# A ring of eight places for the one-hot matrices in place of four, in a two-layer graph network on one core

## The chip, the cores and the metric

The kernel runs on one core of one Trainium2 chip. Times are device microseconds (us). The time before is 308.18 us, the median of three runs (306.78 to 308.36). The trace comes from one further execution, which took 307.07 us.

## The reference, cut to what matters

There are 1024 nodes with 512 features each and 16384 edges, given as `src` and `dst` and sorted by `dst`. The first layer is a masked attention, the second a graph convolution over the same edges:

```
h    = max(layernorm(x), 0)
q, k, v = h @ Wq + bq, h @ Wk + bk, h @ Wv + bv
adj[src, dst] = 1
a    = q @ k.T / sqrt(512), where adj is 1, and -1e6 elsewhere
x    = x + softmax(a) @ v
h    = max(layernorm(x), 0)
h    = agg(h @ W1 + b1)                 # agg: sum over edges, weights dinv[src] * dinv[dst], and loops
h    = relu(batchnorm(h))
x    = x + agg(h @ W2 + b2)
```

Both `adj` and `agg` can be had from one matrix of counts, cnt[dst, src], which says how many edges lead from each source to each target.

## The kernel before, in words

**The counts.** The matrix of counts is made by TensorE (PE). The 128 chunks of 128 edges each are turned into pairs of one-hot matrices: `src_oh` (128 edges x 512 columns, L705) and `dst_oh` (128 edges x 128 columns, for 64 targets in each half of the sources, L707). A matmul of the two (L1055) adds a chunk's edges to the counts of one group of 64 targets. There are 16 groups (`NW`), taken in the order `ORDER`. Since the edges are sorted by target, a group needs only the chunks between two bounds, read into registers (`bounds_of`). A group is worked off in rounds: first one round of two chunks (`LEAD`), then a loop with three chunks a round (`UNROLL`). For groups 3 to 9 ScalarE (ACT) makes the two leading source one-hots instead (`lead_onehots`, L473 and L476), and VectorE (DVE) only the targets' part.

**The ring.** DVE makes the one-hots of a round in one place of a ring, PE uses them. The ring has `RING = 4` places; the place of round k is `k & (RING - 1)`, on both engines. DVE waits until the semaphore `onehots_used` has reached k + 1; PE adds `RING` to it once at the start, and each round's last matmul adds 1. So DVE can be at most four rounds ahead. PE waits until `onehots` has reached k + 1.

**What else runs in this stage.** Between the groups PE makes other products, in the order of `ahead`: before group i it makes the items of `ahead[i]`, such as a block of v (12 matmuls, L989 to L991), a turned block of h (L1023) or a block of q. ACT copies each item's high part from PSUM (L491, L488), DVE the low part (L688, L684). DVE takes the low parts of `ahead[i-2]` just before the one-hots of group i. ACT also copies each group's counts from PSUM (L464), and PE starts group i only once the counts of group i - 2 are copied (`c16`) and, for groups 3 to 9, the leading one-hots are there (`lead_made`). GpSimd (POOL) makes the shifted targets of each group (`drel`, L365) and the columns of the leading chunks (L370). Before group 0 PE has made the turned weights `WT` and three of the four blocks of M = Wq Wk^T; the fourth (`early[11]`) comes after group 0, and the first four blocks of turned h (`early[12:]`) come after group 1.

**Order.** Each engine's order is written out by hand. All waits are on semaphores; nothing is planned by a scheduler.

**Memory.** `src_oh` follows `qk_raw` in a region of 32 KiB a partition; the region behind it is that of `WT`, in which `w_row` lies from 12 KiB on, and `hrow` from 16 KiB on. `dst_oh` shares a region of 4 KiB with `p16`; `hnT` shares another of 4 KiB with `res` and `res_h`.

After the counts come the last blocks of q, the scores and the softmax row by row, the products with v and W1, both aggregations and the product with W2. They use nothing of the ring.

Of the kernel before, what the change touches and what calls it, by code (L numbers as in the profile page):

```python
# [17 lines left out]
P = 128  # L18
N = 1024
# [3 lines left out]
KC = D // P  # L23
NCH = E // P
HALF = 512
# [5 lines left out]
UNROLL = 3  # L31
PAD = 4
ROUNDS = NW * (2 + NCH // UNROLL)
RING = 4
ORDER = (14, 15) + tuple(range(14))
ITEM_BANKS = 6
LOADS = 2
# [14 lines left out]
F32R = mybir.dt.float32r  # L52
BF16 = mybir.dt.bfloat16
F16 = mybir.dt.float16
# [4 lines left out]
def gnn_kernel(nc, x, src, dst, Wq, bq, Wk, bk, Wv, bv, W1, b1, gamma, beta, W2, b2, out):  # L59
    ctx = ExitStack()  # L60

    def sb(name, shape, dt, where=ctx):
        return where.enter_context(nc.sbuf_tensor(name, shape, dt))

    def shared(*groups):

        made = []
        for g in groups:
            s = ExitStack()
            made += [sb(name, shape, dt, s) for name, shape, dt in g]  # L70
            s.close()
        return made

    def hold(name, kib):
        sb(name, [P, 256 * kib], F32)
# [9 lines left out]
        [("qh", [P, NT, 2, KC * P], F32R)],  # L85
        [("qk_raw", [P, 2, KC, D], F32), ("src_oh", [P, RING, UNROLL, HALF], BF16)])
    hold("region_qh", 32)
    WT, pT, h16, h16T, w_row, _, w2, _, hrow, _, w2_raw, g32 = shared(
        [("WT", [P, 2, 2, KC, D], F32R)],
        [("pT", [P, 2, NT, P], F32R), ("h16", [P, 2, D], F16), ("h16T", [P, 2, KC, P], F16), ("w_row", [P, D], F32),  # L90
         ("unused", [P, D], F32), ("w2", [P, 2, KC, D], F32R)],
        [("pT_place", [P, 2, 2, NT, P], F32R), ("hrow", [P, KC, D], F32)],
        [("pT_place2", [P, 2, 2, NT, P], F32R), ("w2_raw", [P, 2, KC, D], F32)],
        [("g32", [P, KC, N], F32)])
# [17 lines left out]

    p16T, drel_second = shared([("p16T", [P, 2, NT, P], F16)], [("drel_second", [P, NW // 2, NCH + PAD], F16)])
    hold("region_p16T", 4)
    dst_oh, p16 = shared([("dst_oh", [P, RING, P, UNROLL], BF16)], [("p16", [P, 2, N], F16)])
    hold("region_dst_oh", 4)
    ecol = sb("ecol", [P, NCH + PAD], F32)
    hnT, res, res_h = shared(
        [("hnT", [P, 2, KC * P], F32R)],
        [("res", [P, HALF], F32R), ("res_h", [P, 2, P], F32R)])  # L120
    hold("region_hnT", 4)
    bias_row = sb("bias_row", [P, 2, D], F32)
    ncol = sb("ncol", [P, NCH + PAD], F32)
    lead_col = sb("lead_col", [P, NW, LEAD], F32)
# [49 lines left out]
    S = {n: ctx.enter_context(nc.semaphore(n)) for n in sem_names}  # L174
# [13 lines left out]
    item_bank = lambda item: start.get(item, final.get(item, 2 + (items.index(item) - len(start)) % ITEM_BANKS))  # L188
    last_in = lambda b, end: max([n for n, other in enumerate(items[:end], 1) if item_bank(other) == b] + [0])

    drel = lambda i: (drel_first if i < NW // 2 else drel_second)[:, i % (NW // 2), :]
    row_of = lambda t: T[:, t // 2, t % 2 * D:(t % 2 + 1) * D] if t < KC else hrow[:, t - KC, :]

# [434 lines left out]
    def _(dve):  # L628
# [70 lines left out]
        def chunks_of(i, c, count, src=True):  # L699

            k = dve.snap(made, min_val=0, max_val=ROUNDS)
            slot = k & (RING - 1)
            dve.wait_ge(S["onehots_used"], k + 1)
            for j in range(count if src else 0):
                dve.tensor_scalar(src_oh[:, bass.ds(slot, 1), j, :].rearrange("p a n -> p (a n)"), iota[:, :],  # L705
                                  ecol[:, bass.ds(c + j, 1)], None, ALU.is_equal)
            dve.tensor_tensor(dst_oh[:, bass.ds(slot, 1), :, 0:count].rearrange("p a n u -> p (a n) u"),  # L707
                              iota_w[:, :, 0:count],
                              drel(i)[:, bass.ds(c, count)].rearrange("p (o u) -> p o u", o=1).to_broadcast(
                                  [P, P, count]), ALU.is_equal).then_inc(S["onehots"], 1)  # L710
            dve.reg_add(made, made, 1)

        def onehots(i, bounds):

            first, end = bounds & (NCH - 1), bounds >> 8
            dve.wait_ge(S["drel_ready"], i + 1)
            chunks_of(i, first, LEAD, not ACT_LEADS <= i < ACT_LAST)
            with dve.Fori(first + LEAD, end, UNROLL) as c:
                chunks_of(i, c, UNROLL)
# [266 lines left out]
    def _(pe):  # L986
# [11 lines left out]
        for a in range(2):  # L998
            m = pe.transpose(bank(1)[:, a * P:(a + 1) * P], ext[:, a:a + 1].to_broadcast([P, P]), ident[:, :])
        m.then_inc(S["ext_ps"], 1)  # L1000
        pe.sem_inc(S["onehots_used"], RING)
        used = pe.alloc_register("used")
        pe.reg_mov(used, 0)

# [41 lines left out]
        def bounds_of(i):  # L1046
            return pe.value_load(lohi[0:1, ORDER[i]:ORDER[i] + 1], min_val=256, max_val=257 * NCH)

        def chunks(i, count, first):

            k = pe.snap(used, min_val=0, max_val=ROUNDS)
            slot = k & (RING - 1)
            pe.wait_ge(S["onehots"], k + 1)
            for j in range(count):
                m = pe.matmul(ps[:, i % 2, :], dst_oh[:, bass.ds(slot, 1), :, j].rearrange("p a n -> p (a n)"),  # L1055
                              lead_oh[:, i % 2, j, :] if first and ACT_LEADS <= i < ACT_LAST else
                              src_oh[:, bass.ds(slot, 1), j, :].rearrange("p a n -> p (a n)"), start=first and j == 0,
                              stop=False, skip_group_check=True)
            m.then_inc(S["onehots_used"], 1)
            pe.reg_add(used, used, 1)  # L1060

        def counts(i, bounds):

            if i >= 2:
                pe.wait_ge(S["c16"], 2 * (i - 1))
            if ACT_LEADS <= i < ACT_LAST:
                pe.wait_ge(S["lead_made"], LEAD * (i - ACT_LEADS + 1))
            first, end = bounds & (NCH - 1), bounds >> 8
            chunks(i, LEAD, True)
            with pe.Fori(first + LEAD, end, UNROLL):  # L1070
                chunks(i, UNROLL, False)
            pe.matmul(ps[:, i % 2, 0:32], zerob[:, :], zerob[:, 0:32], start=False, stop=True,  # L1072
                      skip_group_check=True).then_inc(S["c_done"], 1)
# [17 lines left out]
        for i in range(NW):  # L1091
            for item in ahead[i]:
                make(item)
            now = bounds
            if i + 1 < NW:
                bounds = bounds_of(i + 1)
            counts(i, now)
            if i == 0:
                make(early[11])
            if i == 1:  # L1100
                for item in early[12:]:
                    make(item)
        make(("q", 1, 0))
# [172 lines left out]
```

## Time and profile before

| | us |
|---|---|
| time, median of three runs | 308.18 |
| the profiled execution's own time | 307.07 |
| its span, first to last instruction | 305.2 |
| PE busy | 294.4 (96%) |
| DVE busy | 207.2 (68%) |
| ACT busy | 160.0 (52%) |
| POOL busy | 58.2 (19%) |
| one-hot matmuls, L1055 from `src_oh`, 131 records | 33.0 |
| source one-hots on DVE, L705, 135 records | 40.0 |
| target one-hots on DVE, L707, 35 of 55 records in the largest group | 14.8 |

The granted clock of TensorE is 0.999 of full speed. The profiled execution lasts 1.87 us longer than its span. Starts are in us from the span's start. A row of the timeline merges neighbouring instructions of a line: the start, the time they cover, the engine, the line, what is written and read, how many, and in brackets the engine's idle time before them and what ended it. The bound of a wait named there is inferred by the profiler. Some matmul records are missing (for instance 131 of 135 one-hot matmuls from `src_oh` are there).

### The profile page before, as it was taken

Reading aid. Unit: us, or ns where it says so; the run is one execution under the profiler, and the core shown is the slowest. Engines: PE = TensorE matmul, PEld = TensorE weight load, DVE = VectorE, ACT = ScalarE, POOL = GpSimd, SP = SyncE. Lnnn points to the kernel's source line nnn. Section 1 sums busy time; section 2 is a strip of 40 time slices with the busy share of each in tenths; the row PEclk is TensorE's granted clock in tenths of the full one; section 3 lists DMA queues with packets and bytes.
Section 4 is the critical chain, followed back from the end, with each engine's and each line's share of the span. In section 5 each row is a group of like instructions: output and inputs, shape, how many; then the busy total and the mean of one; then the engine's idle time right before and its main releaser. Section 6 shows DMA issues by size and latency. Waiting matters only on the chain.

```text
span 305.2 us, 4839 instructions
## 1 busy us (share of the span) xinstructions
PE 294.4 (96%) x1339; PEld 227.2 (74%) x1345; DVE 207.2 (68%) x458; ACT 160.0 (52%) x266; POOL 58.2 (19%) x103
## 2 busy tenths in 40 slices
PE   7999889899999999999999999999999999999995
PEld 6777356466665888888888888887888888878884
DVE  3899989999978557965748575568345388276311
ACT  3999967989546546445444554367523044342000
POOL 5351454000000530022131320203010044100000
PEclk9999999999999999999999999999999999999999
DMA  6816040000600309434362625313102000000321
GB/s 250 317 34 176 1 141 0 1 0 2 207 0 3 69 3 240 81 91 95 79 151 40 147 43 104 69 36 69 34 20 52 0 3 0 0 2 0 111 98 69
DMA packets 42312, 21.67 MB, mean 71 GB/s; under 512 B 35760, under 2 KB 36016, under 8 KB 42288
## 3 DMA queue, kind: packets, MB, share of 16 engines
q1 hardware_dynamic: 41744, 20.33, 26.2%
q10 hardware_dynamic: 544, 1.05, 0.9%
q8 instruction: 12, 0.20, 0.3%
q14 instruction: 12, 0.10, 0.1%
HBM read 10.88 MB, written 2.10 MB: 43 GB/s over the span
## 4 chain that ended last, share of the span: by engine, by line
PE 81%; DVE 7%; ACT 4%; DMA 3%; issue 3%; DVEq 1%; ACTq 0%
PE ps L989 18%; PE ps L991 18%; PE ps L990 18%; PE ps L1242 10%; PE ps L1165 8%; PE ps L1055 8%; DMA p16T<-p 2%; DMA qk_raw<-L_gnn_Wk_in 1%; DVE src_oh L705 1%; PE ps L1023 1%; DVE T L809 1%; DVE WT L688 1%; DVE smx L813 1%; DVE dst_oh L707 1%; ACT T L531 1%
## 5 line engine op out<-in xcount | busy, mean ns | idle before, releaser
L705 DVE TENSOR_SCALAR src_oh<-iota,ecol 128x512 f16 x135 | 40.0, 349 | 3.3 <-PE ps L1055 2.8
L1055 PE MATMUL ps<-src_oh,dst_oh 128*128 x131 | 33.0, 381 | 3.9 <-DVE dst_oh L707 3.0
L1165 PE MATMUL ps<-cnt,qh 128*128 128x512 f32 x128 | 30.1, 391 | 0.3 <-ACT cnt L575 0.3
L1055 PEld LDWEIGHTS ps<-src_oh,dst_oh 128*128 x135 | 13.3, 103 | 21.6 <-issue 12.2
L1242 PE MATMUL ps<-qh,cnt 128*128 128x512 f32 x128 | 29.3, 390 | 0.0
L1165 PEld LDWEIGHTS ps<-cnt,qh 128*128 128x128 f32 x128 | 23.9, 188 | 5.6 <-DVE qh L868 0.7
L1242 PEld LDWEIGHTS ps<-qh,cnt 128*128 128x128 f32 x128 | 23.9, 188 | 5.2 <-DVE vb L970 0.3
L991 PE MATMUL ps<-v,pT 128*128 128x512 f32 x64 | 25.0, 390 | 0.0
L989 PE MATMUL ps<-v,pT 128*128 128x512 f32 x64 | 24.9, 390 | 0.0
L990 PE MATMUL ps<-v,pT 128*128 128x512 f32 x64 | 24.9, 390 | 0.0
L989 PE MATMUL ps<-hT,qh 128*128 128x512 f32 x64 | 24.9, 389 | 0.0
L990 PE MATMUL ps<-hT,qh 128*128 128x512 f32 x64 | 24.9, 389 | 0.0
L991 PE MATMUL ps<-hT,qh 128*128 128x512 f32 x64 | 24.9, 389 | 0.0
L403 POOL TENSOR_SCALAR lnb<-bnag 128x1 f32<-128x1 f32 x8 | 7.2, 899 | 81.4 <-DVE bnag L842 81.4
L464 ACT ACTIVATE cnt<-ps 64x512 int16<-64x512 f32 x32 | 18.9, 590 | 5.7 <-PE ps L1072 5.1
L982 DVE SCALAR_TENSOR_TENSOR xt<-ps,dinv,x 128x512 f32<-128x512 f32 x8 | 5.7, 747 | 17.1 <-PE ps L1242 17.1
L531 ACT ACTIVATE T<-T,smx 128x1024 f32<-128x1024 f32 x8 | 9.2, 1154 | 13.7 <-DVE smx L814 13.7
L831 DVE TENSOR_SCALAR pT<-p16T 128x1024 fp32r<-128x1024 f16 x8 | 5.5, 693 | 15.5 <-DMA p16T<-p 15.5
L559 ACT ACTIVATE hnT<-h16T 128x512 fp32r<-128x512 f16 x8 | 5.1, 632 | 20.2 <-DMA h16T<-h 20.2
L498 ACT ACTIVATE T<-zerob,fill 128x1024 f32<-128x1024 bf16 x8 | 9.1, 1147 | 12.4 <-DVE p L821 12.4
L809 DVE COPY_PREDICATED T<-adj,ps 128x1024 f32<-128x1024 int16 x8 | 10.6, 1321 | 7.1 <-PE ps L991 7.1
L707 DVE TENSOR_TENSOR dst_oh<-iota_w,drel_first 128x384 f16 (+1 forms) x35 | 14.8, 422 | 0.6 <-PE ps L1055 0.6
(186 smaller groups left out, 685.0 us busy)
## 6 DMA issues: line engine op xcount, KB each, us to landing
xt<-x_in SPq DMA_DIRECT2D x16, 256.0 KB, 3.2
out<-xt SPq DMA_DIRECT2D x8, 256.0 KB, 2.1
qk_raw<-L_gnn_Wk_in ACTq DMA_DIRECT2D x2, 512.0 KB, 4.9
qk_raw<-L_gnn_Wq_in SPq DMA_DIRECT2D x2, 512.0 KB, 6.8
wB_raw<-L_gnn_Wv_in SPq DMA_DIRECT2D x2, 512.0 KB, 9.0
wB_raw<-L_gnn_W_in SPq DMA_DIRECT2D x2, 512.0 KB, 4.2
w_raw<-L_gnn_W_in SPq DMA_DIRECT2D x2, 512.0 KB, 4.5
bias_row<-L_gnn_b_in SPq DMA_DIRECT2D x2, 256.0 KB, 4.7
```

The costliest lines, as they stand in the source:

```text
L464: act.activation(cnt16[rows, a * KC:(a + 1) * KC, w // 2, :], ps[a * WIN:(a + 1) * WIN, i % 2, :].rearrange("p (s n) -> p s n", n=P), ACT. ...
L498: act.activation(T[:, t % 2, :], zerob[:, 0:1].to_broadcast([P, N]), ACT.Identity, bias=fill[:, t:t + 1]).then_inc(S["mask_set"], 1)
L531: act.activation(T[:, t % 2, :], T[:, t % 2, :], ACT.Exp, bias=smx[:, 1, t:t + 1], scale=SCALE, accum_out=smx[:, 2, t:t + 1]).then_inc(S[" ...
L705: dve.tensor_scalar(src_oh[:, bass.ds(slot, 1), j, :].rearrange("p a n -> p (a n)"), iota[:, :], ecol[:, bass.ds(c + j, 1)], None, ALU.is_ ...
L707: dve.tensor_tensor(dst_oh[:, bass.ds(slot, 1), :, 0:count].rearrange("p a n u -> p (a n) u"), iota_w[:, :, 0:count], drel(i)[:, bass.ds(c ...
L809: dve.copy_predicated(T[:, t % 2, :], adj[:, t % ADJ, :], ps[:, 2 * (t % 2):2 * (t % 2) + 2, :].rearrange("p a n -> p (a n)")).then_inc(S[ ...
L989: pe.matmul(out_, stat(1), mov(0), start=first, stop=False)
L990: pe.matmul(out_, stat(0), mov(1), start=False, stop=False)
L991: return pe.matmul(out_, stat(0), mov(0), start=False, stop=last)
L1055: m = pe.matmul(ps[:, i % 2, :], dst_oh[:, bass.ds(slot, 1), :, j].rearrange("p a n -> p (a n)"), lead_oh[:, i % 2, j, :] if first and ACT ...
L1165: m = pe.matmul(bank(g), qh[:, d, a, c * P:(c + 1) * P], cnt[:, d, n * HALF:(n + 1) * HALF], start=(d == 0 and a == 1), stop=last)
L1242: m = pe.matmul(bank(t), cnt[:, d, t * P:(t + 1) * P], qh[:, d, a, :], start=(d == 0 and a == 1), stop=last)
```

## The change

The ring has eight places from group 2 on; groups 0 and 1 still use four. PE adds 4 to `onehots_used` at the start and 4 more after group 1, before it makes `early[12:]`. `src_oh` grows from 12 to 24 KiB a partition and so reaches over the end of its region into the first 8 KiB of that of `WT`. `dst_oh` grows from 3 to 6 KiB; its region and that of `hnT` become one of 8 KiB, and `ecol` now lies behind it.

```diff
-RING = 4
+RING = 8
+FIRST_RING = 4
...
-    dst_oh, p16 = shared([("dst_oh", [P, RING, P, UNROLL], BF16)], [("p16", [P, 2, N], F16)])
-    hold("region_dst_oh", 4)
+    dst_oh, p16, hnT, _, res, res_h = shared(
+        [("dst_oh", [P, RING, P, UNROLL], BF16)],
+        [("p16", [P, 2, N], F16), ("hnT", [P, 2, KC * P], F32R)],
+        [("p16_place", [P, 2, N], F16), ("res", [P, HALF], F32R), ("res_h", [P, 2, P], F32R)])
+    hold("region_dst_oh", 8)
     ecol = sb("ecol", [P, NCH + PAD], F32)
-    hnT, res, res_h = shared(
-        [("hnT", [P, 2, KC * P], F32R)],
-        [("res", [P, HALF], F32R), ("res_h", [P, 2, P], F32R)])
-    hold("region_hnT", 4)
...
+    ring_of = lambda i: FIRST_RING if i < 2 else RING
...
         def chunks_of(i, c, count, src=True):
-            slot = k & (RING - 1)
+            slot = k & (ring_of(i) - 1)
             dve.wait_ge(S["onehots_used"], k + 1)
...
-        pe.sem_inc(S["onehots_used"], RING)
+        pe.sem_inc(S["onehots_used"], FIRST_RING)
...
         def chunks(i, count, first):
-            slot = k & (RING - 1)
+            slot = k & (ring_of(i) - 1)
             pe.wait_ge(S["onehots"], k + 1)
...
             if i == 1:
+                pe.sem_inc(S["onehots_used"], RING - FIRST_RING)
                 for item in early[12:]:
                     make(item)
```

## Rows read from the trace of the kernel before

**Rows 1.** Busy time by stretch: PE, PEld, DVE, ACT, POOL (instructions), clock, DMA share, GB/s.
```profile
27.40:42.50 15.10, 12.77 (x54) 6.71 (x53) 13.91 (x49) 14.11 (x33) 4.60 (x13) 1.00 0.31 80
...
60.00:87.00 27.00, 26.85 (x122) 17.69 (x123) 26.05 (x83) 20.13 (x40) 0.00 (x0) 1.00 0.18 59
...
99.50:180.00 80.50, 80.50 (x356) 66.22 (x355) 53.38 (x97) 41.66 (x55) 19.53 (x21) 1.00 0.44 95
```

**Rows 2.** Waits from 15 to 100 us: total us, times, longest.
```profile
PE ps L1055 <- DVE dst_oh L707: 3.0, 9, 0.5
DVE src_oh L705 <- PE ps L1055: 2.8, 5, 0.9
...
PE ps L1055 <- ACT cnt L464: 0.7, 1, 0.7
DVE dst_oh L707 <- PE ps L1055: 0.6, 1, 0.6
```

**Rows 3.** Timeline of DVE, groups 2 and 3.
```profile
29.38 0.87 DVE L705 TENSOR_SCALAR src_oh<-iota,ecol 128x512 f16 x3
...
30.51 0.87 DVE L705 TENSOR_SCALAR src_oh<-iota,ecol 128x512 f16 x3
...
32.27 0.88 DVE L705 TENSOR_SCALAR src_oh<-iota,ecol 128x512 f16 x3 [0.56 <-PE ps L1055]
...
40.34 0.88 DVE L705 TENSOR_SCALAR src_oh<-iota,ecol 128x512 f16 x3
...
42.18 0.38 DVE L707 TENSOR_TENSOR dst_oh<-iota_w,drel_first 128x256 f16 x1 [0.63 <-PE ps L1055]
...
46.71 1.01 DVE L705 TENSOR_SCALAR src_oh<-iota,ecol 128x512 f16 x3
47.65 0.50 DVE L707 TENSOR_TENSOR dst_oh<-iota_w,drel_first 128x384 f16 x1
```

**Rows 4.** Timeline of PE, groups 2 and 3.
```profile
31.63 2.97 PE L1055 MATMUL ps<-src_oh,dst_oh 128*128 x13
...
41.81 0.83 PE L1055 MATMUL ps<-src_oh,dst_oh 128*128 x3 [0.33 <-DVE dst_oh L707]
...
46.29 2.95 PE L1055 MATMUL ps<-src_oh,dst_oh 128*128 x12
```

**Rows 5.** Timeline of POOL beside group 3.
```profile
43.31 5.54 POOL L365 TENSOR_SCALAR drel_second<-dcol 128x132 f16<-128x132 f16 x8
```

**Rows 6.** Chain of work that ended last, groups 3 and 5: start, us, what.
```profile
48.41 0.83 PE ps L1055 x3
...
54.70 1.15 ACT lead_oh L476
...
56.53 0.38 PE ps L1055
```

**Rows 7.** Timeline of DVE, groups 14 and 15.
```profile
90.98 0.75 DVE L684 SCALAR_TENSOR_TENSOR qh<-ps,uw,qh 128x512 fp32r<-128x512 f32 x1 [0.73 <-ACT qh L488]
...
94.87 0.88 DVE L705 TENSOR_SCALAR src_oh<-iota,ecol 128x512 f16 x3 [0.73 <-PE ps L1055]
...
98.10 0.41 DVE L707 TENSOR_TENSOR dst_oh<-iota_w,drel_second 128x384 f16 x1
```

**Rows 8.** Timeline of PE, groups 14 and 15.
```profile
95.13 2.04 PE L1055 MATMUL ps<-src_oh,dst_oh 128*128 x8
...
97.10 0.62 PE L1023 MATMUL ps<-ident,uw 128*128 128x128 f32 x4
...
98.81 0.83 PE L1055 MATMUL ps<-src_oh,dst_oh 128*128 x3 [0.54 <-DVE dst_oh L707]
```

**Rows 9.** Timeline of PE's weight loads, groups 5 and 15.
```profile
56.30 0.23 PEld L1055 LDWEIGHTS ps<-lead_oh,dst_oh 128*128 x2 [0.66 <-issue]
57.14 0.41 PEld L1055 LDWEIGHTS ps<-src_oh,dst_oh 128*128 x3 [0.61 <-issue]
...
97.65 0.26 PEld L1055 LDWEIGHTS ps<-src_oh,dst_oh 128*128 x2 [0.17 <-issue]
```

## The prediction, made before the changed kernel was run

> **What bounds the kernel now.** Start with the busy time by stretch [rows 1]. From 99.5 to 180 us PE is busy for 80.50 of 80.50 us, and nothing of the ring is used there: whatever comes earlier at 99.5 us comes earlier at the end. In the stage of the counts this differs from stretch to stretch. From 27.4 to 42.5 us, which is group 2 (12 rounds, the longest group), DVE is busy for 13.91 of 15.10 us and PE for only 12.77. From 60 to 87 us PE is busy for 26.85 of 27.00 us. So the question is only where PE waits for one-hots, and which of these waits a longer ring takes away.
>
> The waits [rows 2] give the ceiling: PE waits 3.0 us for DVE's one-hots, nine times, and DVE waits 2.8 + 0.6 = 3.4 us for a place. These are two sides of different things. A deeper ring makes DVE no faster; it only lets it use time in which it now stands. So the timeline has to say for each wait of DVE whether PE later had to wait for what DVE lost in it.
>
> **Group 2.** DVE starts its rounds while PE still makes two blocks of v. The rounds start at 29.38 and 30.51 us (1.13 apart), and the next, the fifth, not at 31.64 but at 32.27 [rows 3]: the four places are full, and PE takes the first at 31.63 [rows 4]. From there DVE has no gap to the last round, begun at 40.34 (7 rounds on, (40.34 - 32.27) / 7 = 1.153 us each), and PE waits 0.33 us for the last one, which it starts at 41.81 [rows 3, 4]. So DVE bounds the group from the stall to its end. With eight places the fifth round starts at 31.64: 32.27 - 31.64 = 0.63 us is gained, and PE's last round comes at 41.18. PE still waits for most rounds of the group, since a round costs DVE 1.15 us and PE three matmuls of some 0.22 us ((2.97 - 0.38) / 12 from the thirteen of [rows 4], where 0.38 is one matmul [rows 6]). Of the waits of PE, those in this group stay almost entirely.
>
> The gap of 0.63 us at 42.18, which the trace puts down to PE [rows 3], I don't count: it stands before the first round of group 3, and the place it needs was left by the round of PE four before, more than two such rounds before the one at 41.81 [rows 4]. It comes after the loop's end and the read of the next bounds, so I take it to be the sequencer's, and it stays. Were it the ring's after all, it would bring up to 0.14 us (next paragraph).
>
> **Group 3.** PE's last round starts at 48.41 [rows 6], 0.25 us after DVE's last one-hot of it ends (47.65 + 0.50 = 48.15) [rows 3]. DVE's 0.63 us puts it at 47.78. PE's own bound is close: its rounds would begin at 46.29 - 0.63 = 45.66, and nine matmuls of 0.22 us later it could start the last at 47.64 [rows 4]. So the group yields between 0.63 and 48.41 - 47.64 = 0.77 us in all. The spare 0.14 us depends on POOL. Its eight L365 instructions take 43.31 to 48.85 [rows 5], and beside them a round takes DVE 48.15 - 46.71 = 1.44 us instead of 1.13 [rows 3]. If DVE is earlier by 0.63 us, half a round less lies beside POOL, worth up to 0.15 us. I take half: 0.70 us after group 3.
>
> Here the Trainium skill has a rule that says otherwise (SBUF — State Buffer, "Who interferes with whom"): DVE and GpSimd share a port pair that is locked for a whole instruction, and the loser waits. The trace agrees that they hinder each other (1.44 against 1.13 us). By that rule the price goes by POOL instruction and not by time side by side: the same eight meet DVE, wherever it stands, and group 3 gives 0.63 us and not 0.70.
>
> **Groups 4 to 13.** The 0.70 us must be carried by every engine that PE waits for. PE starts group 5 at 56.53, released by ACT, whose second half of the leading one-hots ends at 54.70 + 1.15 = 55.85 [rows 6] (the wait list names another ACT instruction, L464, for these 0.7 us [rows 2]). ACT came to this work from the block of v that PE had just ended, so it moves with PE; the wait stays and the gain passes through. From 60 to 87 us PE has 0.15 us idle in all [rows 1] and needs nothing of DVE that is not there with a margin of over 1 us: DVE is busy for 26.05 of 27 us there, and its own start is also earlier. Here the new places bring nothing and cost nothing. The one risk is ACT, 20.13 us busy.
>
> **Groups 14 and 15.** DVE waits for ACT's copy of a q block until 90.98, which moves with PE. Then it loses 0.73 us to the full ring before the third round of group 14 at 94.87, and so its last one-hot ends at 98.10 + 0.41 = 98.51 [rows 7], and PE, 0.54 us idle, starts its last round at 98.81 [rows 8]. Without the stall the one-hots are ready at 98.51 - 0.73 = 97.78 on the old clock, which is before PE could use them. What then bounds PE is its own sequencer: in group 5, where the data had been there, the next round's weights were loaded 57.14 - 56.30 = 0.84 us after the first round's [rows 9]. From 97.65 [rows 9] this gives 98.49, so 0.3 us earlier than 98.81. Its queue could be better filled than in group 5: two matmuls of 0.22 us give 98.09, so 0.7 us. With neither, 0. I take 0.35, near the first, the nearest row. Group 14's eight matmuls take 2.04 us where 7 x 0.22 + 0.38 = 1.92 would do [rows 8]: between 0 and 0.1, I take 0.05.
>
> **The edits themselves.** The masks with 7 or 3 are the same instruction on each engine. The added semaphore increment on PE is one sequencer operation before the four turned blocks of h; it stands in PE's own queue between instructions that wait for nothing new, and I price it at 0, at most one gap such as the 0.17 us in [rows 9]. It is no new wait either: DVE's group 2 comes behind the low parts of `early[12:]`, which PE makes after the increment. The same order keeps the new places free: they lie over the first 8 KiB of `WT`, read last by the fourth block of M, after group 0. The moved buffers cost nothing, since no instruction or DMA is added. Whether DVE writes as fast over the region's end the trace cannot show; the nearest rows are the round of 1.13 us and the slowest, 1.44 us, and I take 1.13, since POOL explains the other.
>
> **Sum.** 0.63 + 0.07 + 0.05 + 0.35 = 1.10 us. From the profiled execution's own 307.07 us this gives 305.97 us (span 305.2 to 304.1). The median shown, 308.18, is 0.36% above that execution; less the same 1.10 us it is 307.1 us. That is the forecast. From the terms' ends: at least 0.63, at most 0.77 + 0.1 + 0.7 = 1.57, and 1.73 if DVE's pitch in group 2 were 1.13 instead of 1.153 over seven rounds (0.16).
>
> **The rivals.**
> - *Only a part arrives.* Group 2's 0.63 us is kept, but the end gives nothing because PE's sequencer, or the copies by ACT of the counts of group 13, take DVE's place; or ACT, whose work fills three quarters of 60 to 87 us [rows 1], keeps its own time and eats some of the 0.70. Gain 0.3 to 0.65, time 307.7. For it: an `issue` gap stands before the weights of nearly every drained round [rows 9]. Against it: ACT's work hangs on what PE has ended.
> - *More arrives.* All upper ends and the pitch: 1.73 us, time 306.5. For it: PE's queue would be fuller in group 15. Against it: four terms at their best at once.
> - *Nothing.* The Trainium skill (Perfetto Trace Analysis, "Identifying the Most-Contended Engine") says to speed up the engine with the highest share first, which over the span is PE. As a mechanism: PE has so little idle time after 60 us (0.15 of 27 us [rows 1]) that an earlier DVE finds no room, if the gain at 41.8 us is taken back by another wait before 60. Time 308.2. The stretch of group 2, where DVE leads, speaks against it.
> - *Slower.* DVE's writes to places 4 to 7 of the longer buffer take the slow round of 1.44 us. Groups 0 and 1 have two rounds each, so group 2 starts in place 4 and has eight of its twelve rounds in such places: 8 x (1.44 - 1.13) = 2.5 us, less 0.63, so slower by 1.9 us at group 2, and about 0.5 us of this given back at the end: 309.6. It decides from 0.08 us a round on (0.63 / 8). No row shows a speed that depends on the address; the only slow rounds have POOL beside them [rows 5].
>
> **Chances.** Forecast 0.60, a part only 0.20, more 0.11, nothing 0.05, slower 0.04. Half a per cent, about what a measurement can tell from no change, is 1.5 us. The forecast lies within it; the case of more crosses it, and the forecast crosses it if its terms are near their upper ends (a sixth of its chance): 0.11 + 0.10 = 0.21 for faster, 0.04 for slower, 0.75 for the same. For the range: the median less 1.73 is 306.4 and less nothing 308.2; the three runs of before lie 1.58 us apart (306.78 to 308.36), and the median of another three can sit lower by half of that. So 305.8 to 308.3.
>
> **What would show it.** In the trace after: no idle time of DVE before its fifth round of group 2, PE's last round of that group near 41.2 us and PE still waiting some 0.3 us before each; group 3's last round near 47.7; group 5 still released by ACT, now near 55.8; no wait of DVE for PE at group 14; PE's group 15 ending 1.1 us earlier, with an idle gap by `issue` and not by DVE. The prediction is wrong if DVE's rounds in group 2 are over 1.2 us apart, if the 0.70 us at 48 us has shrunk by 60 or by 90 us, or if the gap at 42.18 us goes.

## The result

The changed kernel takes 305.77 us (median of six runs, 304.32 to 306.05), the kernel before 307.62 us in the same comparison (six runs, 306.78 to 308.36). The ratio is 0.9924, 95% interval [0.9904, 0.9945]: faster by 0.8%, some 2.3 us. The start of the program varies by up to 1.5 us from execution to execution (see below), so these few runs give the size only roughly: the two medians alone differ by 1.85 us, while the traces, counted from the end of group 1, show 2.57 us. Two executions, one of the kernel before (601 us) and one of the kernel "changed, all v early" (1688 us), were slow by far and are left out of all ratios. Forecast were 307.1 us, at least 305.8, and most likely "the same". The direction was right. The size forecast, 1.10 us, was less than half of it, and 0.7 us came at a place where the prediction had nothing.

Line numbers have moved by one: DVE's one-hots, L706 and L708, are the L705 and L707 of before; PE's one-hot matmul L1055 is L1056, L989 to L991 are L990 to L992, and a group's closing matmul of 32 columns, L1072, is L1073.

Busy time by stretch, columns as in [rows 1]:

```profile
27.40:42.50 15.10, 13.52 (x58) 7.43 (x58) 14.44 (x53) 14.62 (x36) 4.56 (x12) 1.00 0.28 78
...
60.00:87.00 27.00, 27.00 (x124) 17.62 (x124) 26.48 (x83) 19.69 (x41) 0.00 (x0) 1.00 0.18 59
```

PE has gained 0.75 us of work in the first stretch (in part the first matmuls of what follows group 2, which now begin inside it), and from 60 to 87 us it is as full as before. The waits from 15 to 100 us, which answer to [rows 2]:

```profile
PE ps L1056 <- DVE dst_oh L708: 2.0, 7, 0.3
...
DVE src_oh L706 <- PE ps L1056: 0.7, 2, 0.4
```

DVE waited 2.8 us for a place before, five times, and now waits 0.7 us, twice.

DVE in group 2, which answers to [rows 3]: the fifth round (31.51) follows the fourth (30.39) after 1.12 us, without a gap, and so on to the last (39.42).

```profile
31.51 0.87 DVE L706 TENSOR_SCALAR src_oh<-iota,ecol 128x512 f16 x3
...
39.42 0.87 DVE L706 TENSOR_SCALAR src_oh<-iota,ecol 128x512 f16 x3
...
41.14 0.37 DVE L708 TENSOR_TENSOR dst_oh<-iota_w,drel_first 128x256 f16 x1 [0.52 <-PE ps L1056]
```

PE in groups 2, 3, 14 and 15, which answers to [rows 4, 8]:

```profile
23.63 0.18 PE L1073 MATMUL ps<-zerob 128*128 128x32 bf16 x1
...
40.89 0.83 PE L1056 MATMUL ps<-src_oh,dst_oh 128*128 x3 [0.29 <-DVE dst_oh L708]
...
45.30 2.75 PE L1056 MATMUL ps<-src_oh,dst_oh 128*128 x12
...
93.88 1.89 PE L1056 MATMUL ps<-src_oh,dst_oh 128*128 x8
...
96.10 1.56 PE L1056 MATMUL ps<-src_oh,dst_oh 128*128 x5
```

The twelve matmuls of group 3 now run through (2.75 us, 2.95 before), and so do the eight of group 14 (1.89 us, 2.04 before). The five of group 15 don't: they take 1.56 us where 4 x 0.22 + 0.38 = 1.26 would do, so a pause of some 0.3 us is left between its two rounds, where 0.54 us was.

**A clock that doesn't scatter.** The start of the span is no good origin: group 1 ends anywhere from 23.6 to 25.0 us after it in the traces of this study, whatever the kernel, and that is most of the scatter between runs. The table takes all from the closing matmul of group 1 (23.63 above), by the starts of these closing matmuls (128x32, from `zerob`) in the timelines of PE. The entry of a group is the start of its own closing matmul. "After" is the end of the span less that of group 15, so all that comes behind the counts. "v2 early" and the like are explained with their experiments.

| kernel | ratio to before [95%] | group 2 | group 3 | group 13 | group 14 | group 15 | after |
|---|---|---|---|---|---|---|---|
| before | | 18.74 | 25.34 | 71.36 | 73.26 | 75.73 | 205.7 |
| the same again | 1.0017 [1.0002, 1.0033] | 18.77 | 25.33 | 71.40 | 73.31 | 75.78 | 205.6 |
| changed | 0.9924 [0.9904, 0.9945] | 17.92 | 24.26 | 70.23 | 71.98 | 73.86 | 205.0 |
| the same again | 0.9908 [0.9885, 0.9931] | 17.93 | 24.29 | 70.26 | 72.02 | 73.90 | 205.0 |
| depth 4, eight places | 0.9987 [0.9970, 1.0004] | 18.77 | 25.35 | 71.42 | 73.33 | 75.80 | 205.1 |
| depth 5, eight places | 0.9914 [0.9890, 0.9938] | 17.92 | 24.28 | 70.30 | 72.05 | 73.90 | 205.1 |
| depth 8 in groups 2, 3 | 0.9941 [0.9919, 0.9962] | 17.92 | 24.33 | 70.29 | 72.20 | 74.67 | 205.1 |
| depth 8 from group 12 | 0.9952 [0.9930, 0.9975] | 18.75 | 25.15 | 71.18 | 72.93 | 74.82 | 205.1 |
| before, ecol behind hnT | 0.9970 [0.9953, 0.9987] | 18.78 | 25.34 | 71.45 | 73.36 | 75.83 | 205.1 |
| changed, hnT 32 bytes off | 0.9940 [0.9919, 0.9960] | 17.92 | 24.33 | 70.30 | 72.05 | 73.94 | 205.7 |
| changed, hnT 64 bytes off | 0.9932 [0.9909, 0.9955] | 17.92 | 24.24 | 70.30 | 72.06 | 73.90 | 205.8 |
| changed, v2 early | 0.9979 [0.9962, 0.9997] | 19.62 | 25.71 | 71.87 | 73.63 | 75.47 | 205.1 |
| before, v2 early | 1.0085 [1.0056, 1.0114] | 21.56 | 27.64 | 73.72 | 75.63 | 78.10 | 205.7 |
| changed, all v early | 0.9984 [0.9958, 1.0010] | 19.63 | 25.97 | 71.94 | 73.69 | 75.58 | 205.0 |
| changed, DVE late | one run | 20.17 | 26.69 | 72.69 | 74.44 | 76.33 | 205.0 |

The change gives 75.73 - 73.86 = 1.87 us in the counts and 205.7 - 205.0 = 0.7 us behind them, where nothing uses the ring.

### The profile page after: what moved, and what is told of

The parts are those of the page before. It is cut to its first block, busy times and chain, and to the rows that moved or that the text cites. A ratio compares the mean times of both kernels' runs of the same rounds, so it can differ in the third digit from the quotient of the medians.

```text
span 302.5 us, 4846 instructions
## 1 busy us (share of the span) xinstructions
PE 293.5 (97%) x1345; PEld 227.1 (75%) x1345; DVE 206.5 (68%) x458; ACT 159.8 (53%) x266; POOL 58.2 (19%) x103
## 3 DMA queue, kind: packets, MB, share of 16 engines
q10 hardware_dynamic: 544, 1.05, 0.9%
## 4 chain that ended last, share of the span: by engine, by line
PE 88%; DVE 6%; issue 2%; DMA 1%; ACT 1%; DVEq 1%; ACTq 0%
PE ps L990 20%; PE ps L991 20%; PE ps L992 20%; PE ps L1244 10%; PE ps L1056 9%; PE ps L1167 8%; DMA qk_raw<-L_gnn_Wk_in 1%; PE ps L1024 1%; DVE src_oh L706 1%; DVE WT L689 1%; DVE T L810 0%; DVE cnt L875 0%; DVE smx L814 0%; DVE p L822 0%; DVE dst_oh L708 0%
## 5 line engine op out<-in xcount | busy, mean ns | idle before, releaser
L706 DVE TENSOR_SCALAR src_oh<-iota,ecol 128x512 f16 x135 | 40.1, 350 | 1.2 <-PE ps L1056 0.7
L1056 PE MATMUL ps<-src_oh,dst_oh 128*128 x135 | 33.4, 381 | 2.5 <-DVE dst_oh L708 2.0
L1056 PEld LDWEIGHTS ps<-src_oh,dst_oh 128*128 x135 | 13.3, 103 | 19.8 <-issue 9.7
L992 PE MATMUL ps<-v,pT 128*128 128x512 f32 x64 | 24.9, 389 | 0.0
L991 PE MATMUL ps<-v,pT 128*128 128x512 f32 x64 | 24.9, 389 | 0.0
L990 PE MATMUL ps<-v,pT 128*128 128x512 f32 x64 | 24.9, 389 | 0.0
L990 PE MATMUL ps<-hT,qh 128*128 128x512 f32 x64 | 24.9, 389 | 0.0
L991 PE MATMUL ps<-hT,qh 128*128 128x512 f32 x64 | 24.9, 389 | 0.0
L992 PE MATMUL ps<-hT,qh 128*128 128x512 f32 x64 | 24.9, 389 | 0.0
L708 DVE TENSOR_TENSOR dst_oh<-iota_w,drel_first 128x384 f16 (+1 forms) x35 | 14.6, 416 | 0.5 <-PE ps L1056 0.5
```

The source lines that it names most:

```text
L990: pe.matmul(out_, stat(1), mov(0), start=first, stop=False)
L991: pe.matmul(out_, stat(0), mov(1), start=False, stop=False)
L992: return pe.matmul(out_, stat(0), mov(0), start=False, stop=last)
```

## The experiments

**Is it the ring at all, and how much is scatter?** Both kernels once more, unchanged.

> The kernel before once more, unchanged, so that two profiles of it stand beside that of the change. The sum of the prediction gave 1.1 us; the two traces show 1.98 us at the end of the counts (last matmul of group 15 starts at 97.49 where it started at 99.47) and 2.7 us over the span. Theory A (all of it comes from the ring): here group 15 ends within 0.2 us of 99.5 again, group 2 shows the fifth-round gap of about 0.56 us, and the rounds after it are again 1.15 us apart. Theory B (part of it is scatter between executions): group 15 ends earlier or later by 0.5 us or more, or the rounds are 1.13 us apart. Time: same as before, ratio 0.998 to 1.002.

> The changed kernel once more. Starts are taken from the end of group 1, which lies at 23.6 to 25.0 us in the six traces so far. If the 1.9 us in the counts are the ring's, group 15 ends 73.9 us after group 1 again (75.7 to 75.8 in the two traces of the kernel before and in the one with depth 4), and the rounds of group 2 are 1.13 us apart (1.15 in those three). If that was scatter, 74.3 or more, or 1.15. Ratio to before about 0.992.

Every entry of the table repeats within 0.1 us. The 1.87 us are no scatter, nor is the 0.7 us behind; the ratio of the kernel before to itself, 1.0017 with an interval that leaves out 1, shows that a whole run is known to some 0.2% only. So the experiments are read by the table and not by their ratios.

**Depth or layout.**

```diff
+    short = lambda i: 0 if i < 2 else 4
...
-            dve.wait_ge(S["onehots_used"], k + 1)
+            dve.wait_ge(S["onehots_used"], k + 1 + short(i))
```

This is depth 4: DVE may run only four rounds ahead, though the ring has eight places. For depth 5 `short` gives 3 in place of 4, for depth 8 in groups 2 and 3 alone it is `0 if i < 4 else 4`, and for depth 8 from group 12 on `0 if i < 2 or i >= 12 else 4`.

> The changed kernel with its eight places and its memory, but from group 2 on DVE waits until it is at most four rounds ahead, as before. It tells the depth from the layout. If the depth does it all: the time of before, ratio 0.998 to 1.002, group 15's end at about 99.5 us, DVE's stalls at the fifth round of group 2 (0.6 us) and at the third round of group 14 (0.7 us) back, rounds in group 2 1.15 us apart. If places over the turned weights or the moved buffers have a share, that share stays: rounds of 1.13 us after the stall, and group 2 earlier by 0.16 us than before.

> Eight rounds ahead in groups 2 and 3 only, four from group 4 on. The gain up to the end of group 3 should be kept as in the change: group 3's last matmul (of 32 columns) at about 47.9 us against 49.1. At the end of the counts, if the terms of the prediction are apart from one another, 1.2 of the 1.98 us: group 15's end near 98.2. Time ratio about 0.996. If the first gain is lost again later (theory: it is only the place where DVE waits), group 15 ends at 99 or later.

> Four rounds ahead until group 11, eight from group 12 on. Only the terms at the end: the prediction had 0.40 us for them (0.05 + 0.35), the two traces show 0.8 us (0.21 in group 14 and 0.52 to 0.58 in group 15). So group 3 ends as before (49.1), group 15 at 98.7 if 0.8 is right, at 99.1 if 0.4 is. Time ratio 0.997 to 0.999.

With depth 4 the counts are those of before to 0.1 us, so the places over the turned weights cost and bring nothing there. The two partial kernels split the gain. Groups 2 and 3 give 75.73 - 74.67 = 1.06 us. The kernel with the depth from group 12 on is 75.73 - 74.82 = 0.91 us ahead at the end, but 0.2 us of that is there at group 3 already (25.15, where the other kernels with four rounds ahead have 25.33 to 25.35), before it differs from them. It is not the depth's: in this one trace DVE's rounds beside POOL fell out shorter. From group 13 on the deep ring gives (75.73 - 71.36) - (74.82 - 71.18) = 0.73 us, the same as the 0.74 of the changed kernel, and so the 0.8 us of the expectation was near and the 0.4 of the prediction too small. The gain of groups 2 and 3 passes through groups 4 to 13 undiminished (25.34 - 24.33 = 1.01 there, 71.36 - 70.29 = 1.07 at group 13). But the depth-4 kernel is 0.6 us faster than before behind the counts. No expectation had that, and the next kernels ask for its cause.

**The 0.7 us behind the counts.** After the softmax each of the eight row blocks of h is multiplied by W1: twelve matmuls a block on the three lines L989 to L991, with a piece of `hnT` (the turned h, high or low part) as the stationary operand, the one that is loaded as weights. Their durations, min/median/max ns, with the first and the last start, in the kernel before:

```profile
L990 PE MATMUL ps<-wB,hnT x32: 392/396/396, 138.2 to 233.9; 128*128 128x512 f32 x32
L991 PE MATMUL ps<-wB,hnT x32: 395/396/397, 138.4 to 234.2; 128*128 128x512 f32 x32
```

and in the changed one:

```profile
L990 PE MATMUL ps<-wB,hnT x32: 389/389/389, 135.9 to 231.1; 128*128 128x512 f32 x32
```

The lines that are not shown have the same. 96 of them at 7 ns less make 0.67 us. As the profiler models the ends of matmuls, the starts count more: those of one block are (140.51 - 137.94) / 11 = 0.234 us apart in the kernel before, and (140.59 - 138.10) / 11 = 0.226 us in the first of the three kernels below, which also has 389 ns. The diff moved ecol, 528 bytes a partition, from ahead of hnT to behind it; the allocation puts hnT at byte 216736 before (32 off a multiple of 128) and at 216192 after (a multiple of 128). Three kernels change only that:

```diff
 # before, ecol behind hnT
-    ecol = sb("ecol", [P, NCH + PAD], F32)
...
     hold("region_hnT", 4)
+    ecol = sb("ecol", [P, NCH + PAD], F32)
 # changed, hnT 32 bytes off (64 bytes: [P, 16])
-    dst_oh, p16, hnT, _, res, res_h = shared(
+    dst_oh, p16, _, hnT, _, res, res_h = shared(
...
-        [("p16", [P, 2, N], F16), ("hnT", [P, 2, KC * P], F32R)],
+        [("p16", [P, 2, N], F16), ("skew", [P, 8], F32), ("hnT", [P, 2, KC * P], F32R)],
```

> The kernel before, ring of four, with ecol (528 bytes) declared behind the region of hnT and not ahead of it. hnT then starts at a multiple of 64 bytes a partition (216192) and not 32 bytes off one (216736). Theory A: the 96 matmuls with hnT as the stationary operand, 396 ns each in the kernel before and 389 in the changed one and in that with depth 4, cost 7 ns more because of this offset; then they take 389 ns here, the rows of the softmax come 13.60 us apart and not 13.69, and the end lies 0.5 to 0.7 us nearer to group 1's end, 280.8 against 281.4, while the counts stay at 75.7. Theory B: they got faster through the ring or something else in the change; then all stays as before. Ratio 0.998 by A, 1.000 by B.

> The changed kernel with 32 unused bytes between p16 and hnT, so that hnT starts 32 bytes off a multiple of 64 again; nothing else differs. Theory A (the offset): the hnT matmuls take 396 ns, the rows come 13.69 us apart, and the end lies 0.5 to 0.6 us later than in the changed kernel, 279.4 after group 1's end against 278.9; the counts stay at 73.9. Theory B (some other effect of the layout): 389 ns, 13.60 and 278.9.

> The changed kernel with 64 unused bytes between p16 and hnT: hnT starts at a multiple of 64 bytes that is not one of 128 (216256). If 64 bytes are the step that matters, the hnT matmuls take 389 ns and the rows come 13.60 us apart, as in the changed kernel; if it is 128, 395 ns and 13.69, as with the 32 bytes.

The kernel before with ecol behind:

```profile
L989 PE MATMUL ps<-wB,hnT x32: 389/389/389, 138.1 to 233.3; 128*128 128x512 f32 x32
```

The changed one with 32 bytes, and with 64:

```profile
L990 PE MATMUL ps<-wB,hnT x32: 392/395/396, 136.2 to 231.9; 128*128 128x512 f32 x32
```
```profile
L990 PE MATMUL ps<-wB,hnT x32: 393/396/398, 137.2 to 233.0; 128*128 128x512 f32 x32
```

The offset is shown as the cause, by taking it from the kernel before and by giving it to the changed one, where nothing but hnT moves: the column "after" goes to 205.1 with the one and back to 205.7 and 205.8 with the others, and the counts don't move. My guess of 64 bytes as the step was wrong: 64 off a multiple of 128 costs the same 7 ns. The 0.7 us have nothing to do with the ring, and a reordered declaration alone gives 205.7 - 205.1 = 0.6 us (the ratio of 0.9970 says 0.9 us, within what a ratio is known to).

**How deep, and why the rounds' pitch changed.** The pitch is the time from one round's start to the next. Between the stall of [rows 3] and the end of group 2 the rounds of before are 1.153 us apart, those of the changed kernel (39.42 - 31.51) / 7 = 1.130.

> Eight places, DVE at most five rounds ahead from group 2 on. In group 2 only the fifth round waited for a place, and PE takes the first round just then, so one place more should be enough: group 2 ends 17.9 us after group 1, as with eight. The rounds after it tell two theories of the pitch apart. A: DVE's sequencer lost its lead over the engine at the stall, and works at 1.15 us a round when it has none; without a stall the pitch is 1.13, as with eight. B: the pitch depends on the distance to a place that PE is reading; with five it stays near 1.15 and group 2 ends at 18.1. At groups 14 and 15 one place more takes the 0.73 us stall away but perhaps not all: group 15's end between 73.9 and 74.3. Ratio 0.992 to 0.994.

Depth 5 is depth 8 in every entry, within 0.1 us. Its rounds in group 2 are 1.13 us apart (31.66 to 40.70, eight rounds). So five rounds ahead are enough for this order of the work. A ring of five places was not built; with the place taken as `k & (RING - 1)`, eight is the next count that can be. For the pitch it left one question, answered by a stall without a short ring:

```diff
+            if i == 2:
+                dve.wait_ge(S["item_ps"], nth(("v", 0, 0)))
             onehots(i, now)
```

> The changed kernel, in which DVE waits before its first round of group 2 until PE has made the block v0, some 1.4 us later than it would start by itself. It still may run eight rounds ahead and no place is ever missing. Theory A (DVE's sequencer loses its lead at any stall and then needs 1.15 us a round): the rounds of group 2 come 1.15 us apart though the ring is deep, and the group ends 1.6 to 1.7 us later than in the changed kernel (17.9 after group 1's end): 19.5 to 19.6. Theory B (the pitch belongs to the ring of four places ahead): 1.13 us apart, group 2's end at 19.3.

```profile
29.54 0.62 DVE L706 TENSOR_SCALAR src_oh<-iota,ecol 128x512 f16 x2 [1.81 <-PE ps L994]
30.38 0.88 DVE L706 TENSOR_SCALAR src_oh<-iota,ecol 128x512 f16 x3
...
41.94 0.88 DVE L706 TENSOR_SCALAR src_oh<-iota,ecol 128x512 f16 x3
```

(41.94 - 30.38) / 10 = 1.156 us with eight places ahead. So the pitch goes with a stall and not with the depth: a stall costs its own length and then 0.02 to 0.03 us for each round until the end of the group (one trace; the six other traces of group 2 with four rounds ahead show the same 1.15 after their stall). Nor is it PE that slows DVE by waiting right behind it, since in the changed kernel PE does so for the last five rounds and DVE keeps to 1.13. That DVE's sequencer has lost its lead over the engine is the reading that fits; no row shows the lead itself. The group ended 2.25 us late and not 1.7, since DVE began 1.90 us late (5.63 us after group 1's end and not 3.73), not 1.4; the other 0.35 us are the pitch.

**Can the depth buy more?** In the changed kernel PE still waits for DVE at the last five rounds of group 2. Three kernels move blocks of v ahead of earlier groups.

```diff
-    [("v", 0, 0), ("v", 1, 0)], [("v", 2, 0), ("h", 4, 0)], [("v", 3, 0), ("h", 5, 0)],
+    [("v", 0, 0), ("v", 1, 0), ("v", 2, 0)], [("h", 4, 0)], [("v", 3, 0), ("h", 5, 0)],   # v2 early
 # all v early, from group 2 on: [v0, v1, v2], [v3, h4], [h5, h6], [h7, v4], [v5], [v6], [v7], []
```

> The changed kernel with the block v2 (12 matmuls, 2.7 us) made before group 2 and not before group 3. In the changed kernel PE still waits some 0.3 us for each of the last five rounds of group 2. With v2 ahead of it, PE comes 2.7 us later to the group, finds eight rounds ready and works them off at its own 0.68 us a round: group 2 ends 0.5 us later than in the changed kernel (18.4 after group 1's end) with v2 already made, so group 3 waits for DVE instead: its last one-hot bounds it, end 0.3 to 0.4 us earlier (23.9). Group 4 has one more low part ahead of it on DVE and may give some of it back. Group 15 at 73.5 to 73.7 against 73.9. The rival (DVE's added low part and ACT's added copy fall on the path) gives 73.9 or more.

> The same move of v2 in the kernel before, ring of four. Here DVE stands still after four rounds until PE has made v2 as well, so its fifth round of group 2 starts 2.4 us later than in the kernel before and all the rest of the group with it: group 2 ends at 21.2 after group 1's end and not 18.7, group 3 at 27.6 and not 25.3, group 15 near 78 against 75.8. Slower than before, ratio 1.007. It shows what the depth buys: an order of the work in which PE comes late to the long group. The rival (the stall is worked off within group 3, since v2 is no longer there) gives group 15 at 76.

> The changed kernel with v2 before group 2, v3 before group 3, two turned blocks of h before group 4, the last of them and v4 before group 5, and v5 to v7 one group earlier each, so that group 9 has no item. v4 then covers PE's wait for ACT before group 5 (0.4 us) and the sequencer gaps in it (0.7 us), and v3 the wait that v2 alone would uncover in group 3. Group 5 should end about 1.4 us earlier in the sum of work done, and group 15 at 72.5 to 73.0 against 73.9, unless DVE, which is busy for 26.5 of 27 us from 60 to 87 us, becomes the bound there: then 73.3 or later. Ratio to before 0.987 to 0.990.

Both with the deep ring fell 1.6 to 1.7 us behind the changed kernel in the counts; both expectations were wrong. PE in group 2 of the first of them, after v2:

```profile
35.65 4.91 PE L1056 MATMUL ps<-src_oh,dst_oh 128*128 x22
40.74 0.83 PE L1056 MATMUL ps<-src_oh,dst_oh 128*128 x3 [0.18 <-issue]
...
43.97 0.83 PE L1056 MATMUL ps<-src_oh,dst_oh 128*128 x3 [0.26 <-issue]
```

DVE's last one-hot of the group ends at 42.01, 1.96 us before PE starts on it, and still PE does a round only every 1.05 to 1.09 us. The idle time is by `issue`: after the first 22 matmuls the sequencer's 1.08 us a round is the bound ((43.97 - 40.74) / 3), and the 0.68 us of three matmuls is not. (That the sequencer had prepared the first ones during the block of v is the reading of this; no row shows it.) So in group 2 PE's own limit is only 0.05 us a round below DVE's 1.13, and there was next to nothing to fill. The trace of the kernel before had this pace already, in group 5, before which PE has only eight short matmuls. Its rounds start at 57.15, 58.22 and 59.29, the last two over 1 us after their one-hots were ready (56.85 and 58.23):

```profile
58.22 0.83 PE L1055 MATMUL ps<-src_oh,dst_oh 128*128 x3 [0.25 <-issue]
```

Worse, group 3 lost the block ahead of it: its fourteen one-hot matmuls now take from 45.80 to 50.72, 4.9 us with `issue` gaps between all rounds, where they take 3.0 us in the changed kernel (44.87 to 47.89). Taking v out of one group's front costs there what it covers elsewhere. In the last kernel PE also waits once for 2.0 us (1.96 at 76.45) for ACT's leading one-hots, where group 9 has no item ahead. With the ring of four, v2 early is 2.4 us slower than before, as expected: in that order of the work the deeper ring is worth 78.10 - 75.47 = 2.6 us in the counts, of which 1.87 are what it gives in the old order.

No kernel tried beats the changed one. That with depth 5 is its equal.

## Why the prediction was too small, step by step

The forecast rested on two things: a sum of 1.10 us for the counts, and nothing for the moved buffers. The first was too small by 0.77 us, the second by 0.7.

- **Group 2: the stall.** Right: 0.63 us predicted, the gap is gone, and PE still waits some 0.3 us for each of the last five rounds. The pitch of 1.153 us was kept in the sum and its 0.16 us put only into the upper end; it came. 0.82 us in all (18.74 - 17.92). The prediction had no reason for the slower pitch, and the kernel with DVE late shows one: the stall itself.
- **The gap of 0.63 us at 42.18** [rows 3]. Right in the main: it stays (0.52 us at 41.14, 0.11 shorter), though the ring is deep and the trace still names PE.
- **Group 3.** 0.07 us predicted beyond group 2, measured 25.34 - 24.26 - 0.82 = 0.26. Two of DVE's four rounds with source one-hots now escape POOL (41.65, 42.82, 43.97: 1.17 and 1.15 us) and PE becomes the bound, with its twelve matmuls in 2.75 us. The prediction let only DVE move. Counted from group 1, DVE starts these rounds 0.93 us earlier (42.69 - 23.74 = 18.95, now 41.65 - 23.63 = 18.02), and POOL its eight instructions 0.50 us later (19.57 in [rows 5], now 20.07), as in the eight traces in which DVE runs freely through group 2; why POOL comes later is open:

```profile
43.70 5.44 POOL L366 TENSOR_SCALAR drel_second<-dcol 128x132 f16<-128x132 f16 x8
```

  The price of POOL was also mis-sized: 1.44 us is a round from its first start to its last end, and 1.13 is from start to start. By starts a round beside POOL takes 1.40 (45.32 - 43.92) against 1.15 after a stall. How much of the 0.26 us is the ring's stays open, since the kernel with the depth from group 12 on had 0.2 us of it with four rounds ahead. Of the Trainium skill's rule (SBUF — State Buffer, "Who interferes with whom") one half shows: POOL's hindrance did not vanish, since DVE's first source one-hots of group 4 now take 1.00 us (48.29) and not 0.87. But it fell on rounds that nobody waits for, so group 3 was earlier by more than the 0.63 us that the prediction drew from the rule.
- **Groups 4 to 13.** Right that the gain passes through: 1.08 us at group 3, 1.13 at group 13, and the wait for ACT at group 5 stays (0.43 us). The prediction read 0.66 us there, because the record of that group's first matmul is missing; the repeat of the kernel before shows 0.43, released by `lead_oh`.
- **Group 12.** The longest stall of all, 0.95 us at 86.32, was not in the prediction. It went too, and it brought nothing, because DVE then has to wait for ACT's copy of a block of q: 0.73 us before [rows 7], and twice that now.

```profile
89.73 0.75 DVE L685 SCALAR_TENSOR_TENSOR qh<-ps,uw,qh 128x512 fp32r<-128x512 f32 x1 [1.44 <-ACT qh L489]
```

- **Group 14.** 0.05 predicted, 0.15 measured (1.75 us from group 13 to 14 in place of 1.90). The stall of 0.73 us is gone.
- **Group 15.** 0.35 predicted, 75.73 - 73.26 - (73.86 - 71.98) = 0.59 measured. The prediction let PE's sequencer start from 97.65 [rows 9] as before. But without the stall in group 14 the weights of group 15 are loaded sooner after the turned row (97.65 - 97.10 = 0.55 us before, 95.99 - 95.64 = 0.35 after). The likely reason, which no row shows, is that DVE's stall had also held PE's sequencer at the third round of group 14:

```profile
95.64 0.63 PE L1024 MATMUL ps<-ident,uw 128*128 128x128 f32 x4
...
95.99 0.22 PEld L1056 LDWEIGHTS ps<-src_oh,dst_oh 128*128 x2
96.82 0.41 PEld L1056 LDWEIGHTS ps<-src_oh,dst_oh 128*128 x3 [0.61 <-issue]
```

  From there the 0.83 us to the next round's weights is what the prediction took from group 5 (0.84). DVE is close behind: its last one-hot ends at 96.48, 0.34 us before PE starts on it, where PE in group 2, waiting for DVE, starts 0.27 us behind the one-hot (40.62 to 40.89). So hardly more could have come here, whatever the sequencer did.
- **"The moved buffers cost nothing, since no instruction or DMA is added."** This step failed: a term was put at zero because no instruction was added. Nothing is added indeed, but 96 matmuls changed their duration with the address of an operand, and that is 0.7 us, more than a quarter of the whole.

The sum in the counts: 0.82 + 0.26 + 0.05 + 0.15 + 0.59 = 1.87 us against 1.10; with 0.7 us, 2.57 against 1.10. In the counts the places and the mechanism were right and the sizes too small, most of all the pitch in group 2, POOL in group 3 and the sequencer in group 15. The rival of more, 1.73 us from all upper ends and the pitch, described the counts best, and even it was 0.14 us short of them and 0.84 short of the whole. As to the stated range, the measured 305.77 us lies 0.03 us below its lower bound of 305.8, and that bound was worked out wrongly: 308.18 - 1.73 - 0.79 (half of 1.58) is 305.66. Had the range held by this, it would have been by its allowance for scatter and not by its terms. The baseline also moved: the first three runs of before had a median of 308.18, later groups of runs 307.17 to 308.05.

## What to carry to other kernels

Look not only at what a change of buffers is for, but at which operands of which loops it moves; here the min and max duration of a group of matmuls showed it at once. For each stall of the producer, look at what both engines wait for next: the stalls in groups 2 and 14 cost time, the longest one, in group 12, cost none. One more round ahead was all it took here. Before filling an engine's wait with other work, ask whether its sequencer could go faster if the data were there: rounds elsewhere in the trace, with `issue` before them, give that pace.

## What the runs showed of the hardware

- A 128x512 fp32r matmul of this loop shows 389 ns with its stationary tile at a multiple of 128 bytes a partition, and 392 to 398 ns with it 32 or 64 bytes off; the matmuls start 0.226 and 0.234 us apart. The weight load itself shows 188 ns either way. Only this one tile was moved, and other offsets were not tried.
- PE takes 1.05 to 1.12 us (once 1.25) for a round of three one-hot matmuls with register-addressed operands, a wait and a loop step, with `issue` gaps, though the one-hots are there; the matmuls alone take 0.68 us. Behind a block of matmuls with fixed addresses 22 one-hot matmuls run through without a gap (v2 early). That the sequencer builds up this stock meanwhile is the reading of the `issue` gaps behind them; no row shows it by itself.
- DVE's rounds in group 2 are 1.13 us apart when it runs freely and 1.15 to 1.16 after a stall (of 0.56 to 3.3 us, in seven traces), until the group ends.
- The beginning of the program, before group 1's end, varies by 1.5 us between executions of any of these kernels; from there on a kernel run again repeats within 0.1 us. Group 3, where DVE works beside POOL, can differ by 0.2 us though the program up to there is the same (25.15 against 25.35).
